# Expert weights read in place for the first 128 tokens of each expert, copies for the other blocks, and new costs in the planner of the expert layers

## The reference, cut to what matters

```python
logits = x @ gate_w.T                                  # 2048 x 64 experts
topv, topi = jax.lax.top_k(logits, 8)                  # each token goes to 8 experts
rw = softmax(topv)
W = zeros((N, E)).at[arange(N)[:, None], topi].set(rw)
gu = einsum('nh,eih->nei', x, gu_w)                    # 128 gate and up rows per expert
inter = silu(gu[..., :64]) * gu[..., 64:]
out = einsum('nei,ehi->nh', inter * W[:, :, None], dp_w)
out += sigmoid(x @ sh_gate1_w.T) * (silu(x @ sh_gate_w.T) * (x @ sh_up_w.T)) @ sh_down_w.T
```

## Time and profile before

| What | Value |
|---|---|
| median of three runs | 2062.28 us (2058.95 to 2062.55) |
| the profiled execution | 2058.86 us |
| its span, first to last instruction | 2054.7 us |
| TensorE busy (PE) | 1715.9 us, 84% |
| VectorE busy (DVE) | 1441.0 us, 70% |
| ScalarE busy (ACT) | 1110.3 us, 54% |
| POOL busy | 682.0 us, 33% |
| weight copies on ScalarE (L1191) | 320 of 520 ns, 159.1 us busy |
| weight copies on VectorE (L1947) | 192 of 424 ns, 81.4 us busy |
| gate-and-up products (L1449) | 2048 matmuls, 315.4 us busy |
| down products (L1466) | 2048 matmuls, 197.7 us busy |

### The profile page before, as it was taken

One profiled execution on the slowest core, in us unless ns is written; L12 is line 12 of the kernel. 1 busy time (PEld: TensorE's weight loads), 2 busy tenths in 40 slices (PEclk: granted clock), 3 DMA queues, 4 the chain that ended last, 5 costly groups with the idle time before them and its releaser, 6 DMA issues.

```text
span 2054.7 us, 36352 instructions
## 1 busy us (share of the span) xinstructions
PE 1715.9 (84%) x12410; PEld 1071.6 (52%) x12410; DVE 1441.0 (70%) x3081; ACT 1110.3 (54%) x1975; POOL 682.0 (33%) x764
## 2 busy tenths in 40 slices
PE   6799999999877777988688999999998677779920
PEld 5445454445655656774334454544446566667710
DVE  5688989885766733886437889898848677338843
ACT  2155757667455655663122557575664566556610
POOL 6000101001366354445650001010013663544466
PEclk9788989899988899999895879898899888989965
DMA  7530404000444455665753104030004545546644
GB/s 231 164 60 2 64 2 63 2 2 7 180 170 146 157 165 151 191 196 189 213 174 57 27 2 63 2 63 1 2 7 180 180 148 162 160 146 200 201 151 117
DMA packets 127905, 225.94 MB, mean 110 GB/s; under 512 B 15364, under 2 KB 91028, under 8 KB 123444
## 3 DMA queue, kind: packets, MB, share of 16 engines
q1 hardware_dynamic: 103152, 156.49, 25.2%
q0 software_dynamic: 24576, 67.14, 12.0%
HBM read 124.20 MB, written 98.84 MB: 109 GB/s over the span
## 4 chain that ended last, share of the span: by engine, by line
PE 60%; DVE 11%; issue 9%; DMA 6%; ACT 5%; POOL 4%; another core or an unknown queue 2%; SPq 2%; DVEq 0%; ACTq 0%; POOLq 0%
PE late_banks L1659 13%; PE late_banks L1617 11%; PE late_banks L1449 9%; PE exp_banks L1645 7%; PE exp_banks L1466 6%; POOL ring_t L1043 3%; PE late_banks L1424 3%; DVE chunk_max_t L2076 3%; PE late_banks L1482 2%; PE late_banks L1623 2%; ACT probs_t L1287 2%; DVE inter_t L1957 1%; DMA expert_rows<-outs_t 1%; DVE hot_t L1778 1%
## 5 line engine op out<-in xcount | busy, mean ns | idle before, releaser
L1287 ACT ACTIVATE probs_t<-exp_banks 128x1024 f32<-128x1024 f32 (+3 forms) x640 | 538.9, 896 | 319.7 <-PE exp_banks L1645 317.0
L2076 DVE TENSOR_REDUCE chunk_max_t<-late_banks 128x1 f32<-128x512 f32 (+1 forms) x960 | 601.7, 682 | 99.2 <-PE late_banks L1617 82.6
L1125 POOL TENSOR_SCALAR_AFFINE_SELECT probs_t<-probs_t 128x512 f32<-128x512 f32 x128 | 81.5, 637 | 807.2 <-ACT probs_t L1287 807.2
L1449 PE MATMUL late_banks<-tokensT_t,fetched_t 128*128 x2048 | 315.4, 302 | 30.4 <-ACT fetched_t L1191 22.9
L1038 POOL DMA_INDIRECT ring_t<-token_rows,index_t x256 | 249.8, 976 | 213.0 <-PE late_banks L1424 144.4
L1659 PE MATMUL late_banks<-probs_t,values_t 128*32 128x512 f32 (+3 forms) x2560 | 316.8, 569 | 1.9 <-POOL probs_t L1125 1.1
L1957 DVE TENSOR_TENSOR inter_t<-late_banks,silu_t 64x256 f32<-64x256 f32 x512 | 217.7, 425 | 138.4 <-ACT silu_t L1208 107.4
L1043 POOL DMA_INDIRECT ring_t<-expert_rows,rows_of_t x256 | 244.0, 953 | 203.6 <-DVE x_sb_t L1975 138.7
L1449 PEld LDWEIGHTS late_banks<-tokensT_t,fetched_t 128*128 128x128 f32 x2048 | 270.5, 206 | 61.8 <-issue 44.3
L1466 PE MATMUL exp_banks<-fetched_t,inter_t 64*128 64x128 f32 x2048 | 197.7, 315 | 79.6 <-DVE inter_t L1957 49.5
L1617 PE MATMUL late_banks<-contextT_t,Qp_t 50*128 50x512 f32 (+7 forms) x640 | 233.7, 508 | 8.5 <-DVE chunk_max_t L2076 2.1
(11 more groups left out here) (225 smaller groups left out, 1894.9 us busy)
## 6 DMA issues: line engine op xcount, KB each, us to landing
expert_rows<-outs_t SPq DMA_DIRECT2D x256, 256.0 KB
weights_t<-in_experts SPq DMA_DIRECT2D x8, 1728.0 KB, 13.8
Qp_t<-q_rows SPq DMA_DIRECT2D x12, 768.0 KB
weights_t<-in_experts SPq DMA_DIRECT2D x4, 2112.0 KB, 7.2
q_rows<-part_hi_t SPq DMA_DIRECT2D x16, 512.0 KB, 6.3
...
```

Of the source, the lines that this page charges most:

```text
L1287: act.activation(probs[:, e % NP, 2 * p:2 * p + 2, off:QB], exp_banks[sq % 2][:, :, off:QB], ACT.Exp, scale=D ** -0.5).then_inc(exp_done, 1)
L1449: last = pe.matmul(bank[:, blk * P:(blk + 1) * P], fetched[:, n % NFETCH, blk, k * P:(k + 1) * P], tokensT[:, bass.ds(starts_of[n][blk] + ...
L2076: op = dve.tensor_reduce(chunk_max[:, b, p, chunk_row(r), chunk_col(b, r, c)], bank[:, 0:n].rearrange("q (p k) -> q p k", p=len(parts)), A ...
```

## The change

In each half the first 64 blocks are fixed: block e is the first 128 tokens (or fewer) of expert e, and its weights are read where they lie in `weights`. What an expert has beyond 128 tokens goes to the other 64 blocks ("loose"), whose weights are copied as before. The slots are ordered so: first each expert's first 128 at most, expert by expert, then what is beyond, expert by expert. So pairs 0 to 31 and 64 to 95 of a layer take no copies, and for pairs 32 to 63 and 96 to 127 ScalarE copies the first block's weights and VectorE the second's. The buffers of `fetched` are counted by loose pairs. The wait for the parts of the weights stands on TensorE for the first half's fixed pairs, and before the first loose pair on ScalarE and VectorE. A gate-and-up product waits for tiles up to 2j + 2 instead of 2j + 3.

The map gets more: the tally is split into its first 128 (`own`) and the rest (`over`); keys carry a mark of 32768 from the diagonal of `earlier16`, which takes the place of the mask; tokens beyond the 128th are moved on to the loose columns and rows (`moved`, `row_moves`). POOL sets up more constants.

In the planner the costs of a gate-and-up product, a down product and a turning are raised, and a ScalarE copy item is one copy.

The diff, cut to its core:

```diff
+FIXED = NEXP // 2
+MARK = 32768.0
+MAP_SETS = 13
-OTHER_FROM = NPAIR // 2
+def own_weights(n):
+    return n % NPAIR < FIXED
+def loose_no(n):
+    return n // NPAIR * (NPAIR - FIXED) + n % NPAIR - FIXED
+def loose_pair(v):
+    return v // (NPAIR - FIXED) * NPAIR + FIXED + v % (NPAIR - FIXED)
...
-    COST = {"gather": 1.27, "turn": 0.35, "gate_up": 0.8, "down": 0.5, "index": 0.65, "table": 0.6, "fetch": 1.15,
+    COST = {"gather": 1.27, "turn": 0.4, "gate_up": 1.2, "down": 0.75, "index": 0.65, "table": 0.6, "fetch": 0.58,
...
-               ("act", [("fetch", n) for n in pairs]),
+               ("act", [("fetch", n) for n in pairs if not own_weights(n)]),
-               ("dve", [("other", n) for n in pairs if n >= OTHER_FROM]),
+               ("dve", [("other", n) for n in pairs if not own_weights(n)]),
...
         elif kind == "gate_up":
-            yield "fetch", n, 0.0
-            if n >= OTHER_FROM:
+            if not own_weights(n):
+                yield "fetch", n, 0.0
                 yield "other", n, 0.0
-            yield "store", h * NG + min(2 * j + 2, NG - 1), 0.0
+            elif h == 0 and 2 * j + 1 >= W_SPLITS[-2]:
+                yield "weights", PIECES - 1, LOADED
+                yield "out", LAST_LOAD, LOADED
+            if j == 0 and h == 1:
+                yield "table_out", 1, 0.0
+            yield "store", h * NG + min(2 * j + 1, NG - 1), 0.0
...
         elif kind in ("fetch", "other"):
-            if n >= NFETCH:
-                yield "down", n - NFETCH, 0.0
-            if 2 * n + 1 >= W_SPLITS[-2]:
-                yield "weights", PIECES - 1, LOADED
-                yield "out", LAST_LOAD, LOADED
+            v = loose_no(n)
+            yield "weights", PIECES - 1, LOADED
+            yield "out", LAST_LOAD, LOADED
+            if v >= NFETCH:
+                yield "down", loose_pair(v - NFETCH), 0.0
...
-        halved = 0.5 if item[0] == "fetch" and item[1] >= OTHER_FROM else 1.0
-        free[engine] = done[item] = when + COST[item[0]] * halved
+        free[engine] = done[item] = when + COST[item[0]]
...
+        def expert_weights(n, blk):
+            if own_weights(n):
+                e = 2 * (n % NPAIR) + blk
+                return weights[:, e * EW:(e + 1) * EW]
+            return fetched[:, loose_no(n) % NFETCH, blk, :]
...  experts_pool: also a memset, an iota and two affine_selects
+            pool.iota(own_rows[:, :], [[P, NEXP]], ...)
+            pool.affine_select(out=later[:, :], ...)
+            pool.affine_select(out=earlier16[:, :], in_=earlier16[:, :], compare_op=ALU.not_equal, fill=MARK, base=0,
+                               pattern=[[1, P]], channel_multiplier=-1).then_inc(map_set, 1)
...  experts_act, "fetch"
-                    for blk in range(2 if n < OTHER_FROM else 1):
-                        act.activation(fetched[:, n % NFETCH, blk, :], weights[:, bass.ds(fetches[n][blk], EW)], ACT.Copy)\
-                            .then_inc(fetch_done, 1)
+                    v = loose_no(n)
+                    if v >= NFETCH:
+                        act.wait_ge(down_done, f * PAIRS + loose_pair(v - NFETCH) + 1)
+                    act.activation(fetched[:, v % NFETCH, 0, :], weights[:, bass.ds(fetches[n], EW)], ACT.Copy)\
+                        .then_inc(fetch_done, 1)
...  bases, TensorE
-                for bank, of in ((cols_bank, tally), (rows_bank, block_rows)):
-                    pe.matmul(bank.rearrange("p (t e) -> p t e", t=HT), of[:, :],
-                              earlier[:, :].rearrange("p (o e) -> p o e", o=1).broadcast_to([NEXP, HT, NEXP]),
-                              start=False, stop=True, skip_group_check=True)
+                pe.matmul(cols_bank.rearrange("p (t e) -> p t e", t=HT), own[:, :],
+                          earlier[:, 0:NEXP].rearrange("p (o e) -> p o e", o=1).broadcast_to([NEXP, HT, NEXP]),
+                          start=False, stop=True, skip_group_check=True)
+                pe.matmul(misc[:, OWN_AT:OWN_AT + 1], earlier[:, :], own[:, 0:1], start=True, stop=True)
+                to = misc[:, SLOTS_AT:SLOTS_AT + NEXP]
+                pe.matmul(to, own[:, :], later[:, :], start=True, stop=False, skip_group_check=True)
+                pe.matmul(to, over[:, :], earlier[:, 0:NEXP], start=False, stop=True, skip_group_check=True)
...
+                pe.matmul(misc[:, ROWS_AT:ROWS_AT + NEXP], block_rows[:, :], earlier[:, 0:NEXP], start=True, stop=True)\
...  "gate_up", TensorE
-                    pe.wait_ge(tile_stored, f * 2 * NG + h * NG + min(2 * j + 3, NG))
+                    pe.wait_ge(tile_stored, f * 2 * NG + h * NG + min(2 * j + 2, NG))
+                    for c in range(len(W_SPLITS) - 1):
+                        if n < FIXED and W_SPLITS[c] <= 2 * j + 1 and c not in landed:
+                            landed.add(c)
+                            pe.wait_ge(weights_in[c], 16 * (f + 1))
...
+                        if not own_weights(n):
+                            pe.wait_ge((fetch_done, fetch_other)[blk], loose_no(f * PAIRS + n) + 1)
+                        expert = expert_weights(n, blk)
...  counted, VectorE
+                dve.tensor_scalar(own[:, :], tally[:, :], float(P), None, ALU.min).then_inc(count_step, 1)
+                dve.tensor_scalar(over[:, :], tally[:, :], -float(P), 0.0, ALU.add, ALU.max).then_inc(count_step, 1)
...  column_keys, row_moves, place_keys, VectorE (moved() is one scalar_tensor_tensor of 128x512)
-                dve.scalar_tensor_tensor(out=col_keys[:, :, :], in0=map_banks(h)[0].rearrange("p (t e) -> p t e", t=HT),
-                                         scalar=1.0, in1=mask16[:, tiles, :], op0=ALU.add, op1=ALU.mult).then_inc(keys_done, 1)
+                dve.tensor_scalar(beyond[:, 0, :], map_banks(h)[2][:, SLOTS_AT:SLOTS_AT + NEXP], -float(P), None, ALU.add)\
+                    .then_inc(beyond_set, 1)
+                to = moved(h, 0)
+                dve.tensor_tensor(col_keys[:, :, :], by_tile(map_banks(h)[0]), to, ALU.add).then_inc(keys_done, 1)
+            def row_moves(h):
+                dve.scalar_tensor_tensor(out=beyond[:, 1, :], in0=map_banks(h)[2][:, ROWS_AT:ROWS_AT + NEXP],
+                                         scalar=float((NEXP - 1) * P), in1=own_rows[:, :], op0=ALU.add, op1=ALU.subtract)\
+                    .then_inc(beyond_set, 1)
+            def place_keys(h):
+                to = moved(h, 1)
+                dve.tensor_tensor(to, to, each_tile(own_rows[:, :]), ALU.add).then_inc(moved_on, 1)
+                dve.tensor_tensor(row_keys[h][:, :, :], by_tile(map_banks(h)[1]), to, ALU.add).then_inc(keys_done, 1)
...
             dve.tensor_copy(index[0][:, :], ...).then_inc(index_ready, 1)
+            row_moves(0)
             block_table(0, ...)
             place_keys(0)
             table_out(0, map_banks(0)[2])
             column_keys(1)
+            row_moves(1)
             place_keys(1)
             dve.tensor_copy(bounds[:, :], ...).then_inc(bounds_ready, 1)
```

143 lines of the change are left out of this document (84 added, 59 removed).

## The result

The changed kernel took **2086.55 us** (2079.09 to 2093.55, 4 runs) beside 2060.61 us for the kernel before on the same chip: a ratio of 1.0137 [1.0108, 1.0167]. It is slower, where 2025 us was forecast.

What follows compares the result with a forecast made beforehand. It took TensorE, with gaps from other queues' order and latency, as the bound. 7.6 + 9.7 + 2.7 + 10.9 + 9.3 + 4 − 7 = 37 us off 2058.86 gives 2021.7; plus 3.4 for the median, 2025 us (range 2000 to 2042).

Steps and rivals of the forecast that it cites:

- (c): Second half's first 32 pairs: without copies each second pair falls from 2.07 to 1.73 us, 10.9 us gained; ends 0 and 10.9.
- They move queue order only: Planner's new costs: they only reorder queues, so engine orders should be spaced as TensorE really runs.
- (a): First stretch, pairs 0 to 32: TensorE's waits for copied weights all vanish, 7.6 us gained; ends 0 and 7.6.
- (b): First stretch: half the waits for other ScalarE results (9.7 us) and a quarter for gated products (2.7 us) vanish.
- (d): Second stretch, pairs 32 to 64: a quarter of 37.1 us of waits hidden by order, 9.3 gained; ends minus 10, plus 30.
- (e): Clock in the first two stretches: fewer gaps mean less half speed, 4 us gained; ends minus 8 and plus 12.
- (f): Map before the first gate-and-up product: more VectorE steps cost 3.5 us a layer, 7 lost; ends 4 and 12.
- The moved wait: TensorE's own wait for the last weight load, at the first half's pair 29: 6.8 us of slack, so zero cost.
- Rival 3: Slower: late combining pieces delay the last weight load, which holds TensorE in the first half; 2082 us, chance 0.12.
- Remote gaps: ScalarE's remote waits in the first two stretches: counted as nothing; upper end 14 us if they follow its instruction count.
- Rival 1: TensorE closes its gaps: first two stretches run near its busy time; 75 us gained, 1987 us, chance 0.13.
- rival 2: Copies were hidden anyway: other waits take their place in the first two stretches; 2051 us, or 2062 without (c), chance 0.20.

Runs made afterwards that it cites:

- e7: Changed kernel with the first half's combining steps spread one a pair and three result buffers instead of two: 1950.81 us, 0.9903 of the kernel before.
- e4: The kernel before with only the planner's new, higher costs for a product, a down product and a turning: 1974.73 us, 0.9986 of the kernel before.
- e12: Changed kernel with the first half's combining steps spread one a pair in the planner: 2032.15 us, 0.9907 of the kernel before.
- e9: The kernel before, unaltered, as a run of its own: 2054.83 us, ratio 0.9979.
- e14: Changed kernel with the first half's combining steps spread one a pair and three result buffers, on another chip: 2020.56 us, 0.9835 of the kernel before.

## Why the prediction was wrong

The failed step is **(c)**: "its first 32 pairs own their weights. No copy stands ahead of the gating, so each second pair should fall from 2.07 to 1.73 us", with the ends 0 and 10.9. The timed pair was right as far as it went: e7, on kind B and with two edits more, runs these pairs at 1.73 us. What failed is that (c) kept VectorE's order as it was and took only the copy out, with 0 as its lower end. "They move queue order only" is said of the new costs (which e4 bears out); nowhere does the prediction ask what the planner puts where a copy stood. Taking it out of VectorE's plan let other work in, and that work drives GpSimd. The measured term is −35 us where +10.9 was forecast.

The size of (c) was wrong too, apart from the crowding. With the steps spread (e12 against e9) the stretch goes from 66.2 / 65.0 to 64.8 / 66.0, a gain of 0.4; with a third buffer too (e14) it is 5.9.

Had (c) been put at 0, the sum of 37 would have been 26, or 0.987 of before. The changed kernel with its steps spread, which has every other term, measured 0.9907 [0.9874, 0.9939] on kind A: that is a gain of 19 us where 26 were left in the sum. That these agree within 7 us is luck in part, as the terms below miss in both directions.

The other terms, from the table above:
- **(a)** 7.6 us of waits for copied weights: gone, as said. **(b)** 12.4: the two together were 20 and the first stretch returned 10.6. In layer 0 the wait for turned tiles fell by 2.0 us and that for the down results by 2.0, but 10.8 us of "issue" stand ahead of the turnings. ScalarE is busy for 48.54 us there, not 41: the prediction took the earlier trace rows off as if no copy overlapped another of ScalarE's instructions, and the 27.5 us of copies took only 20 off its busy time. The first stretch is 111.4 and 115.5 us, not 105.
- **(d)** 9.3 us, a quarter of the waits that an order can hide: 13.2 measured. (a), (b) and (d) together were to give 29.3 and gave 23.8. How much of it is the copies' and how much the new costs' isn't parted on kind A.
- **(e)** Clock: 4 us were to come from fewer gaps. Cut at the same pairs, the clock did rise in the first stretch, from 0.86 to 0.89, and stayed at 0.95 in the second. But the mean over the whole run fell from 0.876 to 0.867, and in pairs 64 to 96 from 0.95 to 0.90, where the holes are. In e7, whose TensorE is busy 55.5 of 57 us there, it is 1.00.
- **(f)** The map: 3.5 us a layer forecast, 4.3 and 3.4 measured at the first silu, close. The chain of the earlier trace rows, in the changed kernel:
```profile
594.65 0.69 DVE L1809 SCALAR_TENSOR_TENSOR chosen_t<-exp_banks,beyond_t 128x512 f32<-128x512 f32 x1
595.37 0.69 DVE L1823 TENSOR_TENSOR col_keys_t<-exp_banks,chosen_t 128x512 f32<-128x512 f32 x1
...
597.68 0.69 DVE L1906 TENSOR_TENSOR row_keys_t<-exp_banks,chosen_t 128x512 f32<-128x512 f32 x1
598.29 0.29 DVE L1969 COPY bounds_t<-late_banks 128x136 f32<-128x136 f32 x1
...
599.36 2.07 PE L1499 MATMUL late_banks<-tokensT_t,weights_t 128*128 x8 [3.38 <-DVE bounds_t L1969]
```
- **The moved wait** for the last weight load: zero forecast; over the whole run TensorE waited for loaded weights once, 1.1 us. Rival 3 did not happen, though the time ended on its side.
- **Remote gaps**, left at nothing, with an upper end by which they go with the number of ScalarE's instructions. They did not: its silu and results waited for "remote" 26.4 + 11.9 us in the whole kernel before, 35.5 + 42.9 in the changed one, and 42.3 + 25.9 in e12, which is faster than before. The prediction took them for gaps of no engine of this core, as the profile gives them. They are waits that a semaphore of TensorE's ended (above), and fewer copies on ScalarE did not take them away. The Trainium skill (Runtime: NRT & Kernel Launch, Instruction fetch mechanics) has fetching ahead mostly hidden; no run here shows whether fetching has a part in them.
- Rival 1 (1987) and rival 2 (2051) are out as mechanisms too: copies were not hidden anyway (23.8 us came back), and neither of the first two stretches ran near TensorE's busy time (86.25 of 112 us and 75.93 of 97).
